# Packed value projection, column-tiled own scores and some steps in another order, in a two-layer gated cross-attention kernel

## The reference

```python
x = x + tanh(g_xattn[0]) * L0_xattn(layernorm(x), ctx, ctx)   # 16 heads of 8 channels
x = x + tanh(g_ffn[0])   * L0_ffn(layernorm(x))               # 8 experts, top 2, silu(h)*g, HID 256
x = x + tanh(g_xattn[1]) * L1_xattn(layernorm(x), ctx)
x = x + tanh(g_ffn[1])   * L1_ffn(layernorm(x))               # 8 experts, top 2, R 64

def L1_xattn(e, c):
    Sim = (e @ w1)[:, :, None] + (c @ w2)[:, None, :] + einsum('bid,bjd->bij', e * w3, c) + b_sim
    A = softmax(Sim, axis=2);  hq = A @ c
    Batt = softmax(max(Sim, axis=2), axis=1);  hc = sum_i Batt[i] * e[i]
    return concat([e, hq, e * hq, e * hc]) @ W_qv + b_qv
```

## Time and profile before

| | |
|---|---|
| runs | 515.8, 516.65, 518.7 us |
| profiled execution, own time | 515.37 us |
| its span (first to last instruction) | 513.6 us |
| mean granted TensorE clock | 0.99 |
| PE busy | 473.2 us, 92% |
| DVE busy | 395.6 us, 77% |
| ACT busy | 307.9 us, 60% |
| POOL busy | 220.1 us, 43% |

### The profile page before, as it was taken

How to read it: one execution, slowest core, us unless ns; L and a number is a source line. 1 busy time by engine, 2 the same in 40 slices (tenths; PEclk the granted TensorE clock), 3 DMA queues, 4 the chain that set the end, 5 groups by cost and what they waited for, 6 DMA issues and landing times. The chain is left out here.

```text
span 513.6 us, 13958 instructions
## 1 busy us (share of the span) xinstructions
PE 473.2 (92%) x4366; PEld 384.4 (75%) x4366; DVE 395.6 (77%) x1566; ACT 307.9 (60%) x750; POOL 220.1 (43%) x300
## 2 busy tenths in 40 slices
PE   2688999999999999999899999988998989899997
PEld 1356777777777777778678888757897877787896
DVE  5778888888889889677675667676798886777974
ACT  1567788777777777555456655474544547453553
POOL 3322055555554334456200177472677762214320
PEclk9999999999999999899989999998999999999999
DMA  8701011111111110134465664220000221000011
GB/s 243 301 11 53 13 32 43 37 36 31 36 36 33 33 54 22 38 89 120 122 172 166 175 177 121 80 78 19 26 22 17 58 61 43 12 0 1 2 42 41
DMA packets 45023, 34.60 MB, mean 67 GB/s; under 512 B 5922, under 2 KB 41122, under 8 KB 44708
## 3 DMA queue, kind: packets, MB, share of 16 engines
q1 hardware_dynamic: 30036, 20.55, 13.4%
q0 software_dynamic: 4128, 8.40, 5.8%
q10 hardware_dynamic: 10800, 4.92, 3.4%
HBM read 21.85 MB, written 11.99 MB: 66 GB/s over the span
## 5 line engine op out<-in xcount | busy, mean ns | idle before, releaser
L493 POOL DMA_INDIRECT sent<-xr,rowu x60 | 59.7, 995 | 46.7 <-DVE rowu L1047 28.3
L509 POOL DMA_INDIRECT yg<-done,gidx x64 | 64.0, 999 | 33.8 <-issue 17.3
L1746 PE MATMUL bank<-QK 128*64 128x256 f32 x512 | 70.6, 397 | 7.9 <-ACT QK L625 5.4
L468 POOL TENSOR_TENSOR ve<-mv,half 128x4 f32<-128x4 f32 (+1 forms) x40 | 8.8, 219 | 118.9 <-DVE mv L845 117.8
L637 ACT ACTIVATE PT<-bank 128x512 f32<-128x512 f32 x64 | 36.4, 602 | 32.4 <-PE bank L1712 31.7
L1305 DVE TENSOR_TENSOR act<-sil,bank 128x256 f32<-128x256 f32 x71 | 29.8, 420 | 29.6 <-ACT sil L687 28.0
L1746 PEld LDWEIGHTS bank<-QK 128*64 128x64 f32 x512 | 32.3, 139 | 26.2 <-ACT QK L625 6.8
L924 DVE TENSOR_REDUCE mx<-bank 128x8 f32<-128x512 f32 x64 | 44.0, 687 | 9.2 <-PE bank L1746 9.2
L687 ACT ACTIVATE sil<-bank 128x256 f32<-128x256 f32 x71 | 27.3, 384 | 35.4 <-PE bank L1903 35.3
L1919 PE MATMUL bank<-f0w_s,aT 128*128 x284 | 45.1, 282 | 0.8 <-DVE yb L1311 0.8
L928 DVE TENSOR_TENSOR Pr<-bank,mx 128x512 f32<-128x512 f32 x64 | 43.7, 683 | 1.6
(11 more groups left out here) (264 smaller groups left out, 1256.2 us busy)
## 6 DMA issues: line engine op xcount, KB each, us to landing
xb<-sent SPq DMA_DIRECT2D x71, 64.0 KB
done<-yb ACTq DMA_DIRECT2D x71, 64.0 KB
cT<-ctx_t_dram SPq DMA_DIRECT2D x16, 128.0 KB, 2.2
f0w_s<-f_w_dram SPq DMA_DIRECT2D x1, 2048.0 KB, 11.4
Pr<-ctx_t_dram SPq DMA_DIRECT2D x8, 256.0 KB
QK<-ctx_tok_dram SPq DMA_DIRECT2D x8, 256.0 KB
out_dram<-xs SPq DMA_DIRECT2D x8, 256.0 KB, 2.3
xs<-x_dram SPq DMA_DIRECT2D x2, 512.0 KB, 6.4
```

The source lines that it names most:

```text
L493: nc.gpsimd.indirect_dma_start(sent, bass.IndirectOffsetOnAxis(ap=rowu[:, s, 2 * k + c:2 * k + c + 1], axis=0), rows[:, c, :], None).then_ ...
L509: nc.gpsimd.indirect_dma_start(yg[:, s, j, :], None, done[0:NBH * P, :] if u < UG else done, bass.IndirectOffsetOnAxis(ap=gidx[:, s, j:j + ...
L1746: last = mm(bank[g % 2][L * b:L * (b + 1), 256 * p:256 * (p + 1)], QT[:, s, g, t:t + L], Kb[:, s, :, t:t + L], start=True, stop=True)
```

## The change

- `wv_eo` is packed: 64 columns for even and 64 for odd heads, no zeros between. `a_v` streams 64 columns instead of 128 and writes half of bank 5; `a_vs` is two copies of 64 partitions. What isn't written in `Vb` stays at the zero that POOL writes at the start (1152 columns; the 256 of `wv_eo` and the 16 of `w1c` go).
- On PE `a_at(u-1)` stands ahead of `a_v(u)`.
- SP writes two blocks of zeros in each of steps 16 to 19 instead of one in each of 16 to 23.
- On DVE `r_pos(14)` and `r_own(14)` go from step 5 to step 4 of the block stage; `c_rmx(0)`, `c_nmx(0)` stand ahead of `sums(2,1)` in step 65; `both(3,0)` goes behind `c_ehc(0,0)`.
- On POOL three of the eight fetches of unit 3 stand ahead of `rstd(2,1)`.
- `c_own` uses a weight tile of 32 equal columns and writes chunk c to partitions 32c to 32c+31. The maxima are spread over 32 columns a chunk (`mcol` 128x128), the softmax works on 128 partitions instead of 4, and `c_wt` transposes 128x128.

```diff
-                    last = mm(bank[5][L * e:L * (e + 1), P * b:P * (b + 1)], cT[:, s, L * b:L * (b + 1)],
+                    last = mm(bank[5][L * e:L * (e + 1), L * b:L * (b + 1)], cT[:, s, L * b:L * (b + 1)],
                               wv_eo[:, e, :], start=True, stop=True)
...
-                nc.vector.tensor_copy(Vb[:, s, :, :, 0:16],
-                                      bank[5][:].rearrange("p (b h d) -> p b h d", b=4, d=16)).then_inc(S("a_vs"), 1)
+                for e in range(2):
+                    keys = slice(L * e, L * (e + 1))
+                    last = nc.vector.tensor_copy(Vb[keys, s, :, :, DH * e:DH * (e + 1)],
+                                                 bank[5][keys, 0:2 * P].rearrange("p (b h d) -> p b h d", b=4, d=DH))
+                last.then_inc(S("a_vs"), 1)
...
+                if has(u - 1):
+                    a_at(u - 1)
                 if has(u):
                     a_v(u, s)
                 if has(u + 1):
                     a_s(u + 1, 1 - s, 0)
-                if has(u - 1):
-                    a_at(u - 1)
...
-                if TAIL <= t < TAIL + E:
-                    zero_after(t - TAIL)
+                if TAIL <= t < TAIL + E // 2:
+                    zero_after(2 * (t - TAIL))
+                    zero_after(2 * (t - TAIL) + 1)
...
             fetch(2, range(8))
+            fetch(3, range(3))
             rstd(2, 1, 4)
-            fetch(3, range(8))
+            fetch(3, range(3, 8))
...
                 if t == 4:
                     r_ln(n, n % 2)
-                if t == 5:
                     r_pos(n - 1)
                     r_own(n - 1)
+                if t == 5:
                     kept(n - 1)
...
             c_rsm(0, 0)
-            both(3, 0)
             c_bs(0)
...
             c_ehc(0, 0)
+            both(3, 0)
...
-                nc.vector.tensor_scalar(mcol[:], rmx[:], gate[:, 4:5], None, ALU.add).then_inc(S("c_mcol"), 1)
+                nc.vector.tensor_scalar(mcol[:], rmx[:].unsqueeze(2).to_broadcast([P, 4, 32]), gate[:, 4:5], None, ALU.add).then_inc(S("c_mcol"), 1)
...
                 for c in range(4):
-                    mm(bank[OWN_BANK[u // UG]][0:4, P:2 * P], w1c[:, c, :], xc(u)[:, P * c:P * (c + 1)], start=c == 0, stop=False)
+                    mm(bank[OWN_BANK[u // UG]][32 * c:32 * (c + 1), P:2 * P], w1r[:], xc(u)[:, P * c:P * (c + 1)], start=True, stop=False)
...
-                mm(bank[OWN_BANK[u // UG]][0:4, P:2 * P], mcol[:], ident, start=False, stop=True).then_inc(S("c_mt"), 1)
+                mm(bank[OWN_BANK[u // UG]][:, P:2 * P], mcol[:].rearrange("p c r -> p (c r)"), ident, start=False, stop=True).then_inc(S("c_mt"), 1)
...
-                wait_alone(pe, S("c_wrow"), u + 1)
-                nc.tensor.transpose(bank[OWN_BANK[u // UG]][:, 4:8], wrow[:], cst[0:4, C_ID:C_ID + 4]).then_inc(S("c_wt"), 1)
+                pe.wait_ge(S("c_wrow"), u + 1)
+                nc.tensor.transpose(bank[OWN_BANK[u // UG]][:, 2 * P:3 * P], wrow[:], ident).then_inc(S("c_wt"), 1)
```

More of the change, by code:

```diff
@@ L137, in flamingo @@
         wq_s, wk_s, wv_s, wo_s = (sb(n, [P, D]) for n in ("wq_s", "wk_s", "wv_s", "wo_s"))
-        wv_eo = sb("wv_eo", [P, 2, D])
+        wv_eo = sb("wv_eo", [P, 2, D // 2])
         bqs = sb("bqs", [P, 1])
@@ L231, in flamingo @@
         rsm = sb("rsm", [P, 4])
[L232 to L237, removed]
+        mcol = sb("mcol", [P, 4, 32])
+        bm = sb("bm", [P, 2])
+        brow = sb("brow", [P, 2, L])
+        bs = sb("bs", [P, 2])
+        br = sb("br", [P, 2])
+        wrow = sb("wrow", [P, P])
         wbd = sb("wbd", [P, 4, 2])
@@ L243, in flamingo @@
         ehq = sb("ehq", [P, 4 * P])
-        w1c = sb("w1c", [P, 4, 4])
+        w1r = sb("w1r", [P, 32])
         ehc = sb("ehc", [P, 2, 4 * P])
@@ L418, in _ @@
                 if u == 1:
-                    sp.wait_ge(fill, 11)
+                    sp.wait_ge(fill, 10)
                     for e in range(E):
@@ L454, in _ @@
             nc.gpsimd.memset(rbias[:], 0.0).then_inc(fill, 1)
-            nc.gpsimd.memset(wv_eo[:], 0.0).then_inc(fill, 1)
+            nc.gpsimd.memset(Vb[:], 0.0).then_inc(fill, 1)
             nc.gpsimd.memset(zero[:], 0.0).then_inc(fill, 1)
@@ L459, in _ @@
             nc.gpsimd.memset(QK[:, 0:U4 // 2, :], 0.0).then_inc(fill, 1)
-            nc.gpsimd.memset(w1c[:], 0.0).then_inc(fill, 1)
             pool.dma_start(f0g_s[:], f0_wg).then_inc(ld_f0g, 16)
-            pool.wait_ge(fill, 11)
+            pool.wait_ge(fill, 10)
             def rstd(k, u, n):
@@ L643, in _ @@
             a.wait_ge(prep, 3)
-            a.wait_ge(fill, 11)
+            a.wait_ge(fill, 10)
             def r_xts(v):
@@ L879, in _ @@
             nc.vector.tensor_scalar(rsum[:, 1, :], rowv[:, R_BQV:R_BQV + D], tg[:, 1:2], None, ALU.mult).then_inc(prep, 1)
+            v.wait_ge(fill, 6)
             for s in range(2):
@@ L887, in _ @@
             v.wait_ge(ld_attn, 64)
-            v.wait_ge(fill, 11)
+            v.wait_ge(fill, 10)
             nc.vector.tensor_copy(bvb[:], colv[:, BV:BV + 1].to_broadcast([P, P]))
@@ L892, in _ @@
             for e in range(2):
-                last = nc.vector.tensor_copy(wv_eo[:, e, :].rearrange("p (h e d) -> p h e d", e=2, d=DH)[:, :, e, :],
+                last = nc.vector.tensor_copy(wv_eo[:, e, :].rearrange("p (h d) -> p h d", d=DH),
                                              wv_s[:].rearrange("p (h e d) -> p h e d", e=2, d=DH)[:, :, e, :])
             last.then_inc(prep, 1)
-            nc.vector.tensor_copy(w1c[:].rearrange("p c m -> p (c m)")[:, 0:16:5], colv[:, W1S:W1S + 1].to_broadcast([P, 4])).then_inc(prep, 1)
+            nc.vector.tensor_copy(w1r[:], colv[:, W1S:W1S + 1].to_broadcast([P, 32])).then_inc(prep, 1)
             def split_biases():
@@ L1360, in c_bsub @@
                 v.wait_ge(S("c_bm"), u + 1)
-                nc.vector.tensor_tensor(brow[:], maxima(u), bm[:].unsqueeze(2).to_broadcast([4, 2, L]), ALU.subtract).then_inc(S("c_bsub"), 1)
+                nc.vector.tensor_tensor(brow[:], maxima(u), bm[:].unsqueeze(2).to_broadcast([P, 2, L]), ALU.subtract).then_inc(S("c_bsub"), 1)
             def c_bs(u):
@@ L1373, in c_wrow @@
                 nc.vector.tensor_tensor(wrow[:].rearrange("p (b l) -> p b l", l=L), brow[:],
[L1374 removed]
+                                        br[:].unsqueeze(2).to_broadcast([P, 2, L]), ALU.mult).then_inc(S("c_wrow"), 1)
             def c_wbd(u):
                 v.wait_ge(S("c_wt"), u + 1)
[L1378 removed]
+                nc.vector.tensor_tensor(wbd[:], bank[OWN_BANK[u // UG]][:, 2 * P:3 * P].rearrange("p (c r) -> p c r", r=32)[:, :, 0:2],
                                         cst[:, C_BI:C_BI + 2].unsqueeze(1).to_broadcast([P, 4, 2]), ALU.mult).then_inc(S("c_wbd"), 1)
@@ L1487, in _ @@
                     nc.vector.tensor_scalar(wqv_g[:], wqv_s[:], tg[:, 1:2], None, ALU.mult).then_inc(prep, 1)
+                if t == NB - 6:
+                    c_rmx(0)
+                    c_nmx(0)
                 for u in range(3):
```

5 lines of the change are left out of this document (1 added, 4 removed).

## The result

The changed kernel took 509.97 us (median of 4 runs, 509.32 to 511.61), the kernel before beside it 516.22; the ratio is 0.9875, with a 95% interval of 0.9841 to 0.991. Timed once more in the first experiment it took 508.62 us, ratio 0.9828 (0.979 to 0.9867). The forecast was 507.4 us and −9.2; measured is −6.3 in the first and −9.4 in the second comparison, both times inside the range of 503.0 to 511.8. In the two profiled executions the span fell by 3.9 us only; how much lies in the code and how much in the clock is told further down.

A forecast was written before the change was run, and what follows sets the result against it. The prediction took PE to bound the kernel, with attention's period closing through DVE. Its terms −5.0 − 1.0 + 0.9 − 3.0 + 0.4 − 1.5 gave −9.2 and 507.4 us, with 503.0 to 511.8 for eight in ten.

The forecast's parts named there:

- attention: Attention units: 64-column value matmuls save PE 0.42 us a unit, less longer copies in three units; −5.0 us.
- rank step: Block stage, step 5: moving the rank operations earlier removes PE's 1.09 us wait for `run`; −1.0 us.
- zeros: Block stage: two zeros a step make PE wait 2.2 to 3.4 us by block 20, none at 23; +0.9 us.
- own scores and their followers: Stage c: four column-tile matmuls take 0.28 us instead of 0.88, −3.0; larger transposes and `mcol` cost +0.4.
- start of stage c: `both(3,0)` behind `c_ehc(0)` removes most of PE's 1.23 us wait and brings unit 1 sooner; −1.5 us.
- the prediction's own guard: Attention: PE's third scores need DVE's first subtraction; 0.52 us needed, 0.61 available, so it just passes.
- rival B: Attention: DVE's copies make PE wait for `Pr` in each unit, leaving 0.1 of 0.42; 511.2 us, chance 0.14.
- Price zero: Attention: putting the transposes of `att` ahead of the values costs nothing; 0.3 us a unit if DVE's cover is gone.
- C: Stage c: own scores' column tiles run one after another, so −3.0 becomes 0; 510.5 us, chance 0.09.
- The transposes of `Pc` by at most 2 sooner: Start of stage c: with `both(3,0)` ahead of `rsm(1)`, PE's next `Pc` transposes come at most 2 us sooner.
- D: Half clock behind block 23's stop and stage c's start both go, −3 us; 504.2 us, chance 0.09.
- Rival E: Attention: granted clock falls behind the 18-column matmuls, 1.7 us each; 521.1 us (eight units) to 531.3 (14), chance 0.04.

The follow-up runs named there:

- the first experiment: The changed kernel timed again without an edit: 508.62 us, ratio 0.9828 to the kernel before.
- 9: The changed kernel with `r_pos(14)` and `r_own(14)` on DVE in step 5 of the block stage again: 510.08 us, ratio 0.9896 to the kernel before.
- 3: The changed kernel with one block of zeros a step in steps 16 to 23 again: 509.71 us, ratio 0.9837 to the kernel before.
- 4: The changed kernel with stage c's own scores as before, softmax on 4 partitions: 510.48 us, ratio 0.9864 to the kernel before.
- 8: The changed kernel with `both(3,0)` ahead of unit 0's softmax and unit 3's eight fetches together behind `rstd(2,1)` again: 512.08 us, ratio 0.9878 to the kernel before.
- experiment 2: The changed kernel with the transposes of `att` behind the values and first scores again: 510.09 us, ratio 0.9862 to the kernel before.
- 5: The changed kernel with DVE's two copies to `Vb` behind the first subtraction: 508.74 us, ratio 0.984 to the kernel before.
- 6: The changed kernel with copies to `Vb` behind the first subtraction and transposes of `att` behind the first scores: 508.02 us, ratio 0.9818 to the kernel before.
- 7: The changed kernel with values 128 columns wide and one `Vb` copy again, transposes of `att` still ahead: 514.68 us, ratio 0.9951 to the kernel before.
- experiment 11: The changed kernel with both attention moves, context loads from step 26, zeros one a step from step 15: 506.04 us, ratio 0.9809 to the kernel before.

## Why the prediction was right in direction and too large

Step by step. Attention and zeros are differences between the profiles of before and after, each between the same two events; the other three are read from the experiment that undoes the step (9 against 3, 4 and 8 against after):

| step | forecast | measured |
|---|---|---|
| attention, unit 0 to 15 | −5.0 | −2.5 |
| rank step | −1.0 | −1.1 |
| zeros, block 16 to 30 | +0.9 | +1.6 |
| own scores and their followers | −2.6 | −1.2 to −1.9 |
| start of stage c | −1.5 | −0.7 |

The prediction named its own test: its mechanism would be wrong "if attention brings less than 3 or more than 6". It brought 2.5, and 2.25 with unit 0. So by that test the largest term's mechanism failed, and that the time fell near 507.4 doesn't vindicate the sum of −9.2: the range was wide, and the median of before was raised by its clock, as told below.

**Attention.** The price of the values (0.51) was right, and that units 0, 1 and 12 gain nothing; they lose 0.3, 0.3 and 0.1, where three times 0.1 was forecast. The step that failed is "12 units at 0.42": a unit gained 0.25. Wrong were two small terms beside the values' price. "A row overlaps the next by some 0.07, so 0.70 for 0.61, +0.10" for the copies: they took 0.88, +0.28, as the two stand 0.44 apart: the length of a copy was right (0.42), the overlap wasn't there. With 0.28, the prediction's own guard reads 0.42 + 0.28 = 0.70 needed against 0.61 available, and doesn't pass. That is rival B, of which I had only the harsh form, and it binds where the transposes stand behind the scores (experiment 2). In after PE comes only some 0.26 sooner, the guard passes, and no `<-DVE Pr` wait stands in the steady units. And "Price zero" for the transposes of `att`: the four transposes cost 0.59 together and 0.37 + 0.37 apart. Experiments 2, 5, 6 and 7 show both: 11.62, 11.64, 11.53, 12.05.

**Own scores.** Four column tiles take 0.36, not 0.28: they do run beside each other, so C is out. The step that failed is "how much of it reaches the end": units 4 to 6 were counted right as nothing or nearly so, but units 1 and 2 give 0.3 together where 1.1 to 1.2 was forecast. Span of own scores 1 to 3 without a clock fall: 19.74 with the old form, 19.45 with the new.

**Zeros.** The mechanism was right, both the two large stops and the fall of the clock behind block 23, which is gone after. The stops are 3.66 in place of my 2.2 to 3.4: the landing took 2.1 to 2.3 us (239.74 to 241.90, 243.16 to 245.28, 246.89 to 249.22), the upper end of what I had allowed, and the estimate at that end was 3.4. With the 2.65 to 3.83 of the same list in other profiles, the +1.6 is the upper end of +0.3 to +1.6. A fall can stand behind these stops too: in the profile of experiment 6 the clock is 0.67 at 244 to 248 us.

**Start of stage c.** "The transposes of `Pc` by at most 2 sooner" didn't come, only the wait for `wrow` went (experiment 8).

**Chance in the clock.** The five rows sum to −3.9 to −4.6, the span differs by 3.9 although the attended values of after's unit 0 came 0.7 late in that execution. Of this 0.3 are the two copies; the first value matmuls came 0.4 late, which is not the change's (in the profiles of the other kernels −0.2 to +1.2 against before). The medians differ by more, 6.3 to 9.4. At equal mean clock of 1.0, before spans 511.6 and 511.7 us, after 506.1 and 506.4: 5.4. Those runs have no profile, and where the 0.8 to 1.5 beyond the five rows lies is open. The rest of the medians' difference goes with the clock: the kernel before ran at 0.983 to 0.993 in most runs and after at 0.990 to 1.0. D was thus partly true, though its two places behaved otherwise: the fall behind block 23 went, that at the start of stage c stayed. Windows of after (columns as in experiment 11):

```profile
344.00:348.00 4.00, 3.21 (x27) 2.60 (x28) 3.04 (x10) 2.64 (x11) 1.04 (x1) 0.84 0.08 20
348.00:352.00 4.00, 4.00 (x28) 3.85 (x28) 3.88 (x17) 1.48 (x5) 0.98 (x2) 0.73 0.07 16
```

and in experiment 5, by the same code, it was absent, as in 2, 4, 7 and 9; from own scores 1 to 3 it is 20.45 to 20.63 us with the fall and 19.45 without (with the new own scores), so it costs 1.0 to 1.2:

```profile
342.00:346.00 4.00, 3.21 (x31) 2.87 (x31) 3.25 (x10) 2.45 (x10) 1.17 (x2) 1.00 0.06 20
346.00:350.00 4.00, 3.73 (x32) 3.31 (x30) 3.79 (x17) 2.51 (x7) 1.89 (x2) 1.00 0.06 16
```

Rival E didn't happen in after: from 20 to 208 us every stretch of 4 us in either profile of after has a granted clock of 1.00. (From 208 to 216, where the block stage starts, it is 0.74 to 0.83; in before it is 0.59 at 212 to 216.)

## What to carry to other kernels

Where a step on the path gets shorter, price its neighbours with the same care: a second guard with 0.09 us to spare needs a measured number, not an overlap guessed from another row. When undoing one suspect changes nothing and undoing the other changes nothing, undo both before dropping either. And work that a queue must do in a fixed time is best spread: the same eight blocks of zeros cost 2.7 to 3.8 us of stops in pairs, 1.7 to 1.8 one a step, and 0.9 one a step with no large load among them.

## What the runs showed of the hardware that I had not expected

- Two copies from PSUM of 64 partitions by 256 elements that follow each other take 0.88 us on DVE from start to the next operation's start, one of 128 by 512 takes 0.60. A copy of 64 by 256 takes 0.42, as an operation on 128 by 256 does: half the partitions save nothing.
- A pair of 128x128 transposes with other matmuls behind it costs 0.37 us, four together 0.59: 0.15 more for the split.
- Four matmuls of 128 columns in four column tiles took 0.36 us, one behind another 0.88: 2.4 times. The Trainium skill ("TensorE: Matmul & The Clock Gate", Part 3 on row and column tiling) gives 2.38 times for three tiles of 512 columns; these runs reach that size with four tiles of 128.
- One kernel's own executions differ by up to 2.7 us in span (after: 506.1 to 508.8 in one comparison), with the mean granted clock at 1.0 and 0.992.
- What a fall of the clock cost differed from place to place: nothing at 462 to 466 us of after (0.60), 1.0 to 1.2 us at the start of stage c, 1.3 us in attention (experiment 11).
